# Cross attention with a quantised feed-forward layer: batch 0's operands and W1's first unit transposed by TensorE, W2's first three quotients moved to GpSimd

## What is computed

```python
query = ctx @ Wq.T + bq;  key = ctx @ Wk.T + bk            # 512 x 128
attention = softmax(query @ key.T)                          # 512 x 512
x = x + layernorm(x) @ attention.T
# feed-forward, MXINT8 fake quantisation in blocks of 32
v = bf16(layernorm(x))
h = bf16(layernorm(v) * ln_w + ln_b)
h = bf16(mx_quant(h) @ mx_quant(W1).T + b1)                 # 512 -> 2048
h = gelu(h)
h = bf16(mx_quant(h) @ mx_quant(W2).T + b2)                 # 2048 -> 512
x = x + bf16(v + h)

def mx_quant(x):                                            # per block of 32
    scale = 2 ** (floor(log2(max|x|)) - 6)
    return clip(round(x / scale), -128, 127) * scale
```

## Time and profile before

| | |
|---|---|
| median of 3 runs | 278.35 us (278.34 to 279.96) |
| the profiled execution's own time | 281.02 us |
| its span, first to last instruction | 279.2 us |
| mean granted TensorE clock | 0.936 of full speed |
| busy: PE, DVE, ACT, POOL | 231.1, 245.4, 170.8, 69.0 us |
| DMA queue of SP (q1): packets' time | 60.5% of 16 engines' span |

### The profile page before, as it was taken

The page is one execution under the profiler, slowest core; times in us unless marked ns, Lnnn a source line. Parts: engine busy times, 40 slices in busy tenths (PEclk is TensorE's granted clock), DMA queues, the critical chain, the costliest instruction groups (busy, mean ns, idle before and its releaser), DMA issues.

```text
span 279.2 us, 3196 instructions
## 1 busy us (share of the span) xinstructions
PE 231.1 (83%) x946; PEld 99.0 (35%) x946; DVE 245.4 (88%) x361; ACT 170.8 (61%) x287; POOL 69.0 (25%) x100
## 2 busy tenths in 40 slices
PE   7767569981899575919979697999999789999993
PEld 7323324440344132403434233344444334444431
DVE  3488999996579999999979999999999999877992
ACT  2357147437698567834997979956556554565510
POOL 2058210032002330064030020192123333333400
PEclk9979779997599998886999899999999999999998
DMA  5967999999999995969032225456532555555673
GB/s 164 377 250 160 235 161 245 211 214 241 241 254 205 248 150 97 240 123 181 2 61 53 45 49 96 94 115 150 131 68 65 132 132 132 132 132 115 144 180 127
DMA packets 103077, 42.92 MB, mean 154 GB/s; under 512 B 93844, under 2 KB 96152, under 8 KB 102552
## 3 DMA queue, kind: packets, MB, share of 16 engines
q1 hardware_dynamic: 100224, 35.93, 60.5%
q10 hardware_dynamic: 2360, 6.83, 9.8%
q0 software_dynamic: 480, 0.02, 0.1%
HBM read 15.48 MB, written 4.19 MB: 70 GB/s over the span
## 4 chain that ended last, share of the span: by engine, by line
DVE 52%; PE 17%; ACT 9%; DMA 7%; SPq 5%; POOL 4%; issue 4%; POOLq 0%; DVEq 0%; ACTq 0%
DVE amax L805 14%; PE ps L764 9%; PE ps L754 5%; DVE w_int L848 4%; DVE pf L912 4%; DVE wquant L902 4%; SPq L245 3%; DMA xhl<-pf 3%; DVE vw L995 3%; DVE hq L1000 3%; DMA wst<-in_L_ffn_W 3%; DVE phl L983 3%; DVE wquant L907 3%; DVE stats L959 2%; DVE xhl L988 2%
## 5 line engine op out<-in xcount | busy, mean ns | idle before, releaser
L764 PE MATMUL ps<-w2T,xhl 128*128 128x512 bf16 x256 | 57.9, 379 | 4.8 <-DMA xhl<-pf 4.8
L754 PE MATMUL ps<-w1T,cxT 128*128 128x512 bf16 x256 | 59.7, 388 | 0.0
L586 ACT ACTIVATE wst<-ps 128x1024 bf16<-128x1024 f32 x32 | 31.9, 1017 | 23.9 <-PE ps L754 23.9
L805 DVE TENSOR_REDUCE amax<-phl 128x64 f32<-128x2048 bf16 x16 | 36.5, 2280 | 4.1 <-ACT phl L593 4.1
L703 PE MATMUL ps<-pT,xT 128*128 128x512 f16 x96 | 27.0, 441 | 13.5 <-DMA pT<-phl 13.5
L764 PEld LDWEIGHTS ps<-w2T,xhl 128*128 128x128 bf16 x256 | 24.5, 98 | 36.1 <-DMA xhl<-pf 7.3
L754 PEld LDWEIGHTS ps<-w1T,cxT 128*128 128x128 bf16 x256 | 24.2, 100 | 33.8 <-issue 8.3
L593 ACT ACTIVATE phl<-wst 128x2048 bf16<-128x2048 bf16 x16 | 30.6, 1910 | 1.6 <-DVE wquant L902 0.5
L691 PE MATMUL ps<-qkT 128*128 128x512 f32 x32 | 19.4, 720 | 12.8 <-ACT pf L479 6.7
L703 PE MATMUL ps<-h1q,xT 128*128 128x512 f16 x96 | 25.0, 417 | 4.4 <-ACT xs L507 2.9
L445 POOL TENSOR_TENSOR wst<-wst,vs 128x512 bf16<-128x512 bf16 x12 | 15.4, 1284 | 51.0 <-DVE wquant L907 51.0
(11 more groups left out here) (81 smaller groups left out, 368.5 us busy)
## 6 DMA issues: line engine op xcount, KB each, us to landing
wst<-in_L_ffn_W ACTq DMA_DIRECT2D x6, 1024.0 KB, 7.0
xs<-in_x SPq DMA_DIRECT2D x4, 1024.0 KB, 10.1
out_x<-wst SPq DMA_DIRECT2D x16, 256.0 KB, 2.9
cx<-in_ctx SPq DMA_DIRECT2D x4, 512.0 KB, 6.9
wst<-in_L_ffn_W SPq DMA_DIRECT2D x2, 1024.0 KB, 9.7
xhl<-pf SPq DMA_TRANSPOSE x17, 4.3
xT<-xhl SPq DMA_TRANSPOSE x16, 4.4
lnw<-in_L_ffn_ln_w ACTq DMA_DIRECT2D x1, 256.0 KB, 6.0
```

Of the source, the lines that this page charges most:

```text
L586: act.activation(ys[:, k, 1024 * g:1024 * g + 1024], ps_y[:, 2 * g:2 * g + 2, :], ACT.Copy)\
L754: last = pe.matmul(ps_y[:, c, :], h1T[:, k, t, :], w1T[:, 4 * c:4 * c + 4, t, :], start=False, stop=(t == KT - 1))
L764: last = pe.matmul(ps_z[:, k, :], h2T[:, k, t, :], w2T[:, t, :], start=False, stop=(t == FT - 1))
L805: dve.tensor_reduce(amax[:, a, :], by_block, AX_X, ALU.max, apply_absolute_value=True)\
```

## The change

Five things are done together.

1. Batch 0: the eight DMA transposes of xhl and phl go. PE transposes each tile (eight 128 x 128 float16 blocks, `turn`) into `ps_t`, which lies in the two banks of `ps_pv`, and ACT copies each of the eight tiles (128 x 1024) to `xT` or `pTs[0]` (`turned`). `values(0, t)` waits for these copies; all later counts of `xT_rdy` and `pT_rdy` are one lower. Copies of the identity in float16 and bfloat16 are made by two DVE casts at the start.
2. W1's unit 0: PE transposes its 16 blocks inside `batch(0, 1, 2)` ahead of `values(0, 2)`, into the banks of `ps_qk`, and ACT copies 128 x 2048 (`w1_turned`) between x_plus(0, 1) and p_high(1, 3). `queries_keys(2)` waits for the copy.
3. W2's units 0 to 2: POOL multiplies by the inverse scale in place, in float32 (`w2_over`), and DVE clips and rounds in one instruction from float32 to int16 (`w_round`) in place of w_over and w_clip. Unit 3 stays as it was. `w2_over(b + 1)` stands between `mean_x1(b)` and `factors_x1(b)`.
4. DVE's order: the maxima and w_amax of W1 stand right behind W2's inverse, the tail ahead of W2's block maximum, and p_low(b, 2) and p_low(b, 3) both ahead of W1's quotient.
5. SP: with batch 0's transposes and W1's first one gone, load_x(2) follows load_ctx(2), and batch 1's transposes are next.

```diff
             load_ctx(2)
-            front(0, None, 2)
+            load_x(2)
             front(1, 3, 3)
...
+            def w2_over(u):
+
+                pool.wait_ge(w_step[W2], W_STEPS * u + 4)
+                w = wst[:, W2, :].rearrange("p (b j) -> p b j", j=BLOCK)
+                inverse = mxi[:, W2, :, 0:1].broadcast_to([P, NB, BLOCK])
+                pool.tensor_tensor(w, w, inverse, ALU.mult).then_inc(w_step[W2], 1)
...
                 mean_x1(b)
+                if b + 1 < B - 1:
+                    w2_over(b + 1)
                 factors_x1(b)
 
+            w2_over(0)
             batch(0, 2, None)
...
+            def turned(n, out):
+
+                act.wait_ge(t_ps, n + 1)
+                act.activation(out, ps_t[:, n % 2, :, :], ACT.Copy).then_inc(t_sb, 1)
...
+                act.activation(w1T[:, 0:4, :, :].rearrange("p r k f -> p (r k) f"), ps_wt, ACT.Copy)\
+                   .then_inc(wt_sb, 1)
...
+                if b == 0:
+                    pe.wait_ge(t_sb, 2 * LT)
...
+            def turn(n, source):
+
+                wait(pe, t_sb, n - 1)
+                for c in range(2 * NT):
+                    last = pe.transpose(ps_t[:, n % 2, c, :], source[:, P * c:P * c + P], ident_h[:, :])
+                last.then_inc(t_ps, 1)
...
+                    if b == 0 and t == 2:
+                        turn_w1()
+                    values(b, t)
                 if qk is not None:
+                    if b == 0:
+                        pe.wait_ge(wt_sb, 1)
                     queries_keys(qk)
...
+            def w_round(u):
+                dve.wait_ge(w_step[W2], W_STEPS * u + 5)
+                dve.tensor_scalar(w_int[:, :], wst[:, W2, :], QMAX, None, ALU.min).then_inc(w_step[W2], 1)
...
                 recip(b, 3)
+                x_low(b, 3)
+                recip_scaled(b, 3)
                 p_low(b, 2)
-                recip_scaled(b, 3)
-                x_low(b, 3)
+                p_low(b, NT - 1)
                 w_over(W1, b)
-                p_low(b, NT - 1)
                 w_clip(W1, b)
```

More of the change, by code:

```diff
@@ L534, in v_sums, with w1_turned, first_batch @@
                                accum_out=sums[:, 1, 0, t:t + 1]).then_inc(v_sum, 1)
+            def turned(n, out):
+                act.wait_ge(t_ps, n + 1)
+                act.activation(out, ps_t[:, n % 2, :, :], ACT.Copy).then_inc(t_sb, 1)
+            def w1_turned():
+                act.wait_ge(wt_ps, 1)
+                act.activation(w1T[:, 0:4, :, :].rearrange("p r k f -> p (r k) f"), ps_wt, ACT.Copy)\
+                   .then_inc(wt_sb, 1)
+            def first_batch():
+                for t in range(LT + 1):
+                    if t < NT:
+                        exp(0, t)
+                        x_high(0, t)
+                    if t > 0:
+                        p_high(0, t - 1)
+                        turned((0, 1, 3, 5)[t - 1], xT[:, t - 1, :, :])
+                    if t > 1:
+                        turned((2, 4, 6)[t - 2], pTs[0][:, t - 2, :, :])
+                    if t == 2:
+                        context(1)
+                load_w1(1)
+                query_key(1, 0)
+                query_key(1, 1)
+                turned(7, pTs[0][:, NT - 1, :, :])
+                exp(1, 0)
+                x_high(1, 0)
             def batch(b, front, qk, v):
                 for t in range(LT + 1):
-                    if t < NT and (t > 0 or front == 0):
+                    if t < NT and t > 0:
                         exp(front, t)
@@ L551, in batch @@
                         v_out(v, t)
-                    if t == 2 and b is not None:
+                    if t == 2:
                         load_w2(front)
@@ L557, in batch @@
                     load_w1(front + 1)
-                if b is not None:
-                    x_plus(b, LT - 1)
+                x_plus(b, LT - 1)
                 if qk is not None:
@@ L565, in batch @@
                     x_high(front + 1, 0)
-                if b is not None:
-                    for t in range(LT):
-                        x1_square(b, t)
+                for t in range(LT):
+                    x1_square(b, t)
             context(0)
@@ L707, in values, with turn_x, turn_p, turn_w1 @@
                           start=False, stop=True).then_inc(pv_ps, 1)
+            def turn(n, source):
[3 more added lines that the diff above has]
+                last.then_inc(t_ps, 1)
+            def turn_x(t):
+                pe.wait_ge(x_lo, t + 1)
+                turn((0, 1, 3, 5)[t], xhl[:, t, :, :].rearrange("p a n -> p (a n)"))
+            def turn_p(t):
+                pe.wait_ge(p_lo, t + 1)
+                turn((2, 4, 6, 7)[t], phl[:, t, :, :].rearrange("p a n -> p (a n)"))
+            def turn_w1():
+                pe.wait_ge(c_idb, 1)
+                pe.wait_ge(w_step[W1], W_STEPS)
+                for c in range(4 * KT):
+                    last = pe.transpose(ps_wt[:, c, :], wquant[:, W1, P * c:P * c + P], ident_b[:, :])
+                last.then_inc(wt_ps, 1)
             def batch(b, front, qk):
-                if qk is not None and b is not None:
+                if qk is not None:
                     context(qk)
@@ L729, in _ @@
             energies(0, 1)
-            batch(None, 0, 1)
+            energies(0, 2)
+            pe.wait_ge(c_idh, 1)
+            turn_x(0)
+            energies(0, 3)
+            turn_x(1)
+            turn_p(0)
+            context(1)
+            turn_x(2)
+            turn_p(1)
+            turn_x(3)
+            turn_p(2)
+            queries_keys(1)
+            turn_p(3)
+            energies(1, 0)
+            energies(1, 1)
             pe.wait_ge(c_idx, 1)
```

105 lines of the change are left out of this document (53 added, 52 removed).

## The result

The changed kernel takes 290.56 us (median of four runs, 289.98 to 291.19); the kernel before took 278.64 us in four runs beside it. The ratio is 1.0419, with a 95% interval of 1.0375 to 1.0462: slower by 11.9 us. The forecast was 287.0 us, slower, range 279 to 292.5. The profiled execution took 289.98 us with a span of 288.2 us.

A forecast was written before the change was run, and what follows sets the result against it. DVE, 88% busy, was taken as the bound before, with ACT taking over after the change. Cumulative lateness of 4.2, 5.5, 5.2 and 8.7 us after batches 0 to 3 gave 278.35 + 8.7 = 287.0 us, range 279 to 292.5.

The forecast's parts named there:

- The sign and its mechanism: Whole kernel: slower, chance 0.75, because ACT takes over from DVE and sets the pace in batches 2 and 3.
- Batch 0: First attention batch: ACT's added copies delay the last p_high, so W2's block maximum starts 4.2 us later.
- The copies of PSUM: Batch 0 on ACT: eight added copies of 128 x 1024, each 0.92 us start to start.
- POOL and its port: W2's quotients on POOL: 4.6 us each; x_low on DVE waits 1.2 us for their end in batches 1 and 2.
- The round: DVE's new float32-to-int16 instruction: 1.1 us, so that replacing quotient and clip saves 1.7 us per batch, three times.
- Batch 1: Second attention batch: +1.3 us, so 5.5 late at its end, with negmax(2, 0) at 67.2.
- Batch 2: Third attention batch: ACT takes over and uses up the freed 6.3 us; 5.2 us late at its end.
- Batch 3: Fourth attention batch: tail ahead of negmax(3, 0) leaves ACT idle, then ACT sets the pace; 8.7 us late.
- rival (c): Batches 2 and 3: POOL's quotient, stretched to 7 us or more, delays factors and v_out; +13.5, 292 us, chance 0.12.
- against the median, 278.35 + 8.7: Final step: the 8.7 us worked out on the profiled execution is added to the median of the runs, giving 287.0.
- 6.3 us of DMA-made waits: DVE between 59 and 92 us: late W1 load and DMA transposes cost up to 6.3 us, freed by the change.
- +8.7 goes through to the end: Feed-forward phase: nothing changes after batch 3, so its 8.7 us lateness reaches the kernel's end unchanged.

The follow-up runs named there:

- e8: Kernel before with DVE's two new orders alone (last p_low ahead of W1's quotient, tail ahead of the row maxima), without PE's or POOL's part: 286.93 us, ratio 1.0295.
- e2: Changed kernel with W1's quotient ahead of the last p_low again, in all four batches: 282.32 us, ratio 1.0111.
- e9: Changed kernel with x_low(b, 0) of batches 1 to 3 moved ahead of W1's block maximum: 293.00 us (one run).
- e1: Changed kernel with batch 3's two row maxima ahead of the tail instead of behind it: 290.66 us, ratio 1.0425.
- b0: Kernel before, unedited, run and profiled a second time: 279.11 us (one run).
- e5: As e1, with factors_x1(1) also ahead of the quotient of W2's unit 2 in POOL's queue: 288.28 us, ratio 1.0330.
- e10: Kernel before with ACT's order alone changed in batches 2 and 3 (v_out(v, 0) later, last p_high earlier): 278.05 us, ratio 0.9960.
- e3: Changed kernel with the row maxima ahead of the tail and W1's quotient ahead of the last p_low: 284.01 us, ratio 1.0180.
- e4: Kernel before with PE's transposes alone (batch 0 and W1's first unit), old DVE orders, no POOL quotient: 281.78 us, ratio 1.0123.
- e6: Changed kernel with the edits of e5 and e2 together: 281.54 us, ratio 1.0090.
- e7: Kernel before with W2's first three quotients on POOL, in orders where nobody waits for them, without PE's part: 280.74 us, ratio 1.0057.
- e11: Kernel before with e10's ACT order and e7's part, one pair of the tail ahead of the two row maxima: 278.26 us, ratio 0.9985.

## Why the prediction was right, and where it was off

**The sign and its mechanism held.** In the changed kernel ACT, not DVE, sets the pace of batches 2 and 3 (DVE waits 18.3 us for it), and e8 and e2 show that the orders which put DVE behind ACT are what cost.

**Batch 0** was foreseen at +4.2 against the first profile; W2's block maximum came at 37.88, +3.84. The copies of PSUM were right (0.90 us start to start, 0.92 taken), and the last p_high stood at 29.71 where 30.3 was worked out.

**POOL and its port** were mis-sized. The quotient was taken at 4.6 us, four times the 1.15 of a 128 x 512 operation; it takes 3.64. So the wait of x_low, 1.2 us in batches 1 and 2, did not occur, though such a wait exists (e9). The round was taken at 1.1 us and measures 1.22:

```profile
L940 DVE TENSOR_SCALAR w_int<-wst x3: 1219/1220/1221, 47.9 to 115.1; 128x2048 int16<-128x2048 f32 x3
```

On the port the Trainium skill ("Advanced Engine Details and Errata", VectorE Performance Modes, Mode Summary) has GpSimd and two-port vector instructions block each other. e9 agrees in effect, and for DVE's side alone, 2.15 instead of 0.74 us with POOL's 3.64 unchanged; the section does not say whether x_low's form, with two tensors in SBUF, counts as one of them. Its "GPSIMD Engine Reference", Performance versus the Vector engine, has 4.50 us for two float32 tensors of 2048. Here 3.64 us was measured, with the second operand one value per block, and the measurement decides.

**Batch 1** was put at +1.3, hence negmax(2, 0) at 67.2; it came at 65.80. The wait ahead of the last p_low was 1.66 us where 1.8 was foreseen. Of the 1.4 us, 0.4 come from batch 0 (+3.84 for +4.2) and about 1 is the port wait that did not occur. **Batch 2**: v_out(0, 0) at 72.44 (6.64 after negmax, foreseen 6.6), the last p_high at 87.28, 14.84 later (foreseen 15.0), the tail at 95.39 (96.7). **Batch 3**: negmax at 104.11 (105.5), v_out(1, 0) at 110.78 (112.5), the last p_high at 124.71 (126.5), W2's maximum at 131.54 (133.1). From the second batch on the walk is right to about 0.4 us a step, on a base 1.4 too late. That it named the tail ahead of the maxima as the reason of batch 3's loss was half of it: e1 shows POOL's queue to be a second, sufficient one, which stood there only as rival (c) with another mechanism, a stretched quotient.

**The profiled execution was met to 0.3 us in part by luck:** 289.7 was forecast and 289.98 measured. At W2's block maximum of batch 3 the changed kernel is 7.2 us later than in the first profile of before, not 8.7 (131.54 against 124.38), and at the first block maximum of gelu's output 7.5, not about 9 (155.61 against 148.08). The port wait that did not occur and a loss in the feed-forward phase that nobody foresaw nearly cancel.

**The median missed by 3.6 us, mostly because of a step that was only arithmetic:** "against the median, 278.35 + 8.7". The difference of 8.7 was worked out against an execution with 6.3 us of DMA-made waits and was then added to a median. b0, 0.5 us above its median, has none of these waits. Against b0 the change costs +9.3 us at W2's maximum of batch 3 (131.54 against 122.24) and +10.9 at the end. That the profiled execution was 2.7 above its own median was written down, but it was not asked what those 2.7 us consist of. b0's marks answer it: 2.1 us of them lie before 125 us, in the stretch with the DMA waits. That the other executions behind the median have none of them either is inferred, from b0 and the four further profiles named with it.

**"+8.7 goes through to the end" did not hold either.** From the first block maximum of gelu's output to the last, the changed kernel takes 115.9 us and b0 114.7. Of the lost 1.2 us, 0.7 are at the start of that phase (6.71 us from the first of these maxima to the second, 6.05 in b0), on PE. First the changed kernel, then b0: PE's first operations on W1 after the attention phase.

```profile
150.67 0.61 PE L836 MATMUL ps<-b1row,ones 3*128 3x512 bf16 x4 [4.35 <-ACT wst L633]
151.22 5.00 PE L841 MATMUL ps<-w1T,cxT 128*128 128x512 bf16 x16
```

```profile
141.65 0.40 PE L749 MATMUL ps<-b1row,ones 3*128 3x512 bf16 x4 [1.49 <-ACT wst L586]
141.98 3.63 PE L754 MATMUL ps<-w1T,cxT 128*128 128x512 bf16 x16
```

The same sixteen matmuls take 5.00 us instead of 3.63. Windows of 2 us near their start show the granted clock (PEclk, the last figure but two), first in the changed kernel, then in b0:

```profile
151.60:153.60 2.00, 2.00 (x6) 0.73 (x5) 0.86 (x2) 1.99 (x2) 1.04 (x1) 0.50 1.49 132
```

```profile
141.90:143.90 2.00, 2.00 (x13) 0.90 (x10) 0.84 (x2) 1.97 (x4) 1.04 (x1) 1.00 0.82 157
```

0.50 is the lower level, 1.2 GHz, and 1.00 is 2.4 GHz. PE had stood idle for 4.35 us in the one and 1.49 in the other. Most of the rest, 0.5 us, is lost near 230 us, where the granted clock of the changed kernel falls once more; b0's at the same distance behind gelu's first maximum doesn't. First the changed kernel, then b0:

```profile
229.60:231.60 2.00, 2.00 (x6) 0.72 (x5) 1.97 (x2) 0.93 (x1) 1.92 (x2) 0.50 0.04 7
```

```profile
219.90:221.90 2.00, 2.00 (x11) 0.78 (x8) 1.97 (x3) 0.22 (x1) 1.46 (x2) 1.00 0.00 0
```

## What to carry to other kernels

Before an engine is relieved, ask in each stage which wait would end last if it were faster, and profile the kernel before a second time: the waits to be freed must be there in the execution that the median stands for. Where an in-order engine waits for a slower one's last link, keep an independent instruction in front of the wait; moving a 2.2 us quotient behind it in each of four batches cost 8 us here. A long operation put on a lightly used engine delays the short ones behind it, which may be links of the real chain.

## What was not expected

PE's clock at the entry of the feed-forward phase decides 1.3 to 2.3 us of PE's time there, of which less reaches DVE (0.7 us in the changed kernel). In the changed kernel, e1, e5, e8, e9 and e10 PE waited 2.8 to 4.4 us, the granted clock fell to 0.50 before or during the sixteen matmuls, and they took 4.9 to 5.9 us. In the first profile of before and in b0, e2, e3, e4, e6, e7 and e11 PE waited 1.1 to 2.4 us, the clock stayed at 1.00, and they took 3.63 in every one. From gelu's first block maximum to its last it is 115.8 to 116.0 us in the six, 114.4 to 115.2 in the eight. In e10 the matmuls take 5.31 us, and this is part of what became of its gain: its attention phase is shorter, but its gelu stretch is 115.9 us against b0's 114.7. That the wait causes the lower clock is inferred from these fourteen traces, and was not tried by itself.

POOL's float32 product of 128 x 2048 took 3.64 us where four operations of 128 x 512 by the earlier trace rows would take 4.6, so scaling up that row overstated this operation by 1 us. Whether the broadcast operand (one value per block) or the length makes the difference was not tried.
